# One AdaLN transformer kernel: the down product in three split passes for eight more units, and its weights split a chunk earlier

## The reference, cut to what matters

```python
scores = softmax(xf @ router_w)                     # 8 experts, the two best are kept
g = einsum('nh,ehf->enf', xf, gate_w)
u = einsum('nh,ehf->enf', xf, up_w)
y = einsum('enf,efh->enh', silu(g) * u, down_w)
routed = einsum('enh,ne->nh', y, combine)
shared = silu(xf @ shared_gate_w) * (xf @ shared_up_w) @ shared_down_w
return shared + routed
```

## Time and profile before

| | us |
|---|---|
| median of 3 runs | 518.63 (518.32 to 519.63) |
| the profiled execution, whole | 518.72 |
| its span | 516.9 |
| TensorE busy | 501.3 (97%), 1941 instructions |
| VectorE busy | 423.4 (82%) |
| ScalarE busy | 390.3 (76%) |
| GpSimd busy | 261.7 (51%) |

### The profile page before, as it was taken

How to read it: one execution, slowest core, us unless ns; L and a number is a source line. 1 busy time by engine, 2 the same in 40 slices (tenths; PEclk the granted TensorE clock), 3 DMA queues, 4 the chain that set the end, 5 groups by cost and what they waited for, 6 DMA issues and landing times.

```text
span 516.9 us, 8074 instructions
## 1 busy us (share of the span) xinstructions
PE 501.3 (97%) x1941; PEld 300.4 (58%) x1941; DVE 423.4 (82%) x1624; ACT 390.3 (76%) x586; POOL 261.7 (51%) x307
## 2 busy tenths in 40 slices
PE   8789999999999999999999999999989999999997
PEld 6345555555555555555555555555546576666675
DVE  5888888988898888888888888898888566876854
ACT  4768888888888888888888888888888753445353
POOL 3445555556656566655555665656655530213242
PEclk9999999999999999999999999999999999999999
DMA  8200010001000100100010001000000000707070
GB/s 246 96 16 1 7 42 15 0 5 41 15 5 15 25 15 5 31 25 0 5 41 15 0 5 41 15 5 21 20 1 1 1 1 1 178 6 184 1 183 22
DMA packets 19526, 17.51 MB, mean 34 GB/s; under 512 B 8604, under 2 KB 14236, under 8 KB 19508
## 3 DMA queue, kind: packets, MB, share of 16 engines
q1 hardware_dynamic: 18644, 16.58, 12.6%
q10 hardware_dynamic: 864, 0.73, 0.4%
HBM read 9.96 MB, written 1.05 MB: 21 GB/s over the span
## 4 chain that ended last, share of the span: by engine, by line
PE 87%; DVE 5%; POOL 3%; issue 2%; ACT 2%; DMA 1%; DVEq 0%; POOLq 0%
PE bank L449 19%; PE bank L440 15%; PE bank L315 12%; PE bank L462 6%; PE bank L607 5%; PE bank L437 5%; PE bank L357 4%; PE bank L362 4%; PE bank L358 4%; PE bank L564 3%; PE bank L563 3%; PE bank L565 3%; DVE hf L1079 1%; PE bank L561 1%; DVE stI L1043 1%
## 5 line engine op out<-in xcount | busy, mean ns | idle before, releaser
L449 PE MATMUL bank<-hid,wf 128*128 128x512 f32 x256 | 120.2, 592 | 0.0
L941 POOL TENSOR_TENSOR rsD<-veD,c_half 128x4 f32<-128x4 f32 x32 | 37.8, 1180 | 118.1 <-DVE veD L1060 118.1
L440 PE MATMUL bank<-x,wf 128*128 128x512 f32 x192 | 93.0, 593 | 0.0
L775 ACT ACTIVATE hid<-bank,vbf 128x512 f32<-128x512 f32 x128 | 77.6, 693 | 1.9 <-PE bank L440 1.9
L449 PEld LDWEIGHTS bank<-hid,wf 128*128 128x128 f32 x256 | 46.1, 190 | 46.6 <-issue 31.3
L440 PEld LDWEIGHTS bank<-x,wf 128*128 128x128 f32 x192 | 35.0, 189 | 33.4 <-issue 16.3
L1150 DVE TENSOR_SCALAR x<-bank,vln 128x256 f32<-128x256 f32 x64 | 31.8, 540 | 23.8 <-PE bank L315 23.8
L1079 DVE TENSOR_SCALAR xhB<-bank,meanB,rsB 128x128 f32<-128x128 f32 x128 | 43.7, 405 | 9.1 <-POOL rsB L941 9.1
L1079 DVE TENSOR_SCALAR xhD<-bank,meanD,rsD 128x128 f32<-128x128 f32 x128 | 43.7, 404 | 7.1 <-POOL rsD L941 2.9
L745 ACT ACTIVATE g<-bank,vbf 128x512 f32<-128x512 f32 x31 | 21.4, 689 | 35.8 <-PE bank L449 35.8
L315 PEld LDWEIGHTS bank<-ident,y 128*128 128x128 f32 x256 | 29.4, 140 | 26.4 <-POOL y L961 12.8
(11 more groups left out here) (185 smaller groups left out, 1118.4 us busy)
## 6 DMA issues: line engine op xcount, KB each, us to landing
wf<-in_w_f SPq DMA_DIRECT2D x16, 256.0 KB, 2.6
hid<-kv_full SPq DMA_DIRECT2D x12, 256.0 KB, 4.3
x<-kv_full SPq DMA_DIRECT2D x9, 256.0 KB, 5.0
wu<-in_w_unit SPq DMA_DIRECT2D x10, 192.0 KB
wqkv<-in_w_qkv SPq DMA_DIRECT2D x7, 192.0 KB, 2.4
x<-in_x SPq DMA_DIRECT2D x4, 256.0 KB, 5.4
qk<-kv_full SPq DMA_DIRECT2D x3, 256.0 KB, 5.0
out<-ot SPq DMA_DIRECT2D x3, 256.0 KB, 2.2
```

Of the source, the lines that this page charges most:

```text
L440: mm = nc.tensor.matmul(ps_ff[j][:], wf1[:, j * P:(j + 1) * P], x2[(c - 2) % CH][:], start=True, stop=True)
L449: mm = nc.tensor.matmul(ps_f0[:], wf2[:, j, :], hid[:, j, :], start=(j == 0), stop=(j == FJ - 1))
L775: nc.scalar.activation(hid[:, j, :], ps_ff[j][:], ACT.Gelu_apprx_tanh, bias=vbf1[:, j:j + 1]).then_inc(h_ready, 1)
L941: nc.gpsimd.tensor_tensor(rs[buf(k, n)][:], ve[buf(k, n)][:], c_half[:], ALU.pow).then_inc(rstd_ready[k], 1)
```

## The change

Down products of the first eight units of the third chunk (units 20 to 27) are done in three passes as well. So split(i) gives 0 to 7 for them, and 8 to 15 for those of the fourth chunk; ScalarE and GpSimd write the high and low parts of 16 instead of 8 tiles sc. The down weights are split in the iterations of the second chunk (c == CH - 3 is c == 1) instead of the third.

```diff
         def split(i):
 
-            return i - (CH - 1) * U if (CH - 1) * U <= i < CH * U - 2 else -1
+            c, u = divmod(i, U)
+            return (c - CH + 2) * (U - 2) + u if c >= CH - 2 and u < U - 2 else -1
...
-                if c == 2 and u < U - 2:
+                if c == CH - 3 and u < U - 2:
                     nc.scalar.activation(wu_hi[:, u, 2, :], wu[:, u, 2, :], ACT.Copy).then_inc(wd_hi_ready, 1)
...
-                if c == 2 and u < U - 2:
+                if c == CH - 3 and u < U - 2:
                     pool.wait_ge(wd_hi_ready, u + 1)
                     nc.gpsimd.tensor_tensor(wu_lo[:, u, 2, :], wu[:, u, 2, :], wu_hi[:, u, 2, :].bitcast(F32),
                                             ALU.subtract).then_inc(wd_lo_ready, 1)
```

## The result

The changed kernel takes 524.5 us (median of 5 runs, 524.23 to 526.26), the kernel before 518.6 (518.32 to 519.63). The ratio is 1.0117, 95% interval 1.0103 to 1.0131: slower by 1.2%. The forecast was 522.4 us, range 520.6 to 524.8. Direction and place were right; the size was 2.1 us short.

A forecast was written before the change was run, and what follows sets the result against it. TensorE, busy 97% of the span, was taken as the bound. Terms of +3.7 and +0.2 us at kk made +3.9, taken as +3.8 on 518.63: 522.4 us, range 520.6 to 524.8.

The forecast's parts named there:

- Three passes: Down products of units 20 to 27: period 2.265 to 2.10 us, -1.32 us in all, -0.50 ahead of the xhF transposes.
- Low parts cost no wait by themselves: New operands: low part ready 0.57 us before its pass, so no wait where nothing else is queued on GpSimd.
- Low part 23 ahead of rsF: Fourth chunk's norm: GpSimd makes rsF late, xhF transposes start 3.8 us later, TensorE stands for 4.3 us.
- the 1.4 named as a sign: Sign in the profile after: VectorE's first product of unit 23 takes 1.4 us.
- From xhF to kk: Between the fourth chunk's xhF and kk transposes: VectorE decides, sum at kk +3.7 us, TensorE waiting some 0.5 us there.
- Weights' splits: Splits moved to the second chunk: hidden except for a conflict with VectorE's first product of unit 17, +0.2 us.
- Fourth chunk: Fourth chunk's buffers, waits and order stay: 0 us.
- The clock: Rival, chance 0.19: TensorE's clock falls in the stall before the xhF transposes, +1.5 us, so 523.9 us.
- the forecast case: Main case, chance 0.72: late rsF stalls TensorE before the fourth chunk's xhF transposes, 522.4 us, 0.7% slower.
- The rule of the Trainium skill quoted there: Rule: a matmul stream that keeps waiting for data drops to half rate and begins the next burst cold; 523.9 us by it.
- RsF has cover: Rival, chance 0.09: at the fourth chunk's norm nbias is less than 1.3 us late, saved passes come through, 517.3 us.
- the point named: Deciding point for covered rsF in the fourth chunk's norm: rsF starts before 474.3.

The follow-up runs named there:

- the stop filled: Changed kernel with 16 float32 128x128 matmuls put on TensorE ahead of the wait for the fourth chunk's xhF: 523.03 us, 1.0086 to the kernel before.
- the low part of hf moved ahead: Changed kernel, GpSimd making the fourth chunk's rsF and nbias ahead of low part 23 and its low part of hf ahead of low part 26: 520.29 us.
- the one tried with all eight: Changed kernel with fourth-chunk norm and low part of hf earlier on GpSimd, statistics and kk earlier on VectorE, units 20 to 27 in three passes: 520.58 us.
- the kernel with rsF ahead: Changed kernel, but GpSimd makes rsF and nbias of the fourth chunk ahead of the low part of unit 23: 520.56 us, 1.0036 to the kernel before.

## Why the prediction held where it did, and what it missed

The 5.70 us of kk to kk split by the experiments: 2.67 us from the place of low part 23 (16.02 - 13.35), 0.71 us left of the way to xhF, 1.57 us from the clock (15.45 - 13.88), and 0.75 us left of the way from xhF (13.88 - 13.13). Each part is a difference of two profiled executions. Outside that stretch there are 0.2 us more.

1. *Three passes.* Right: period 2.10 us, 0.47 us saved ahead of xhF for 0.50 (up 25 ends so much earlier, counted from kk).
2. *Low parts cost no wait by themselves.* Right in the fourth chunk and in units 20 to 22: no wait of TensorE for a low part there.
3. *Low part 23 ahead of rsF.* Right in place and chain; rsF at 477.26 (477.1 forecast), sc of unit 23 late by 0.96 us for 0.75. The stop was 3.68 us for 4.3, xhF +3.41 us for +3.8. Nbias started 1.16 us after rsF, not 1.61, since rsF took 1.01 us, not 1.46. I had taken over the length from before, where VectorE's product of unit 23 (two SBUF inputs) ran beside rsF; here VectorE had nothing to do by then. (In every trace looked at rsF takes 1.46 to 1.50 us with such a product beside it and 1.01 to 1.02 without one.) And the conflict with low part 22 fell on veF, two instructions earlier than I put it; the first product of unit 23 took 0.68 us, not the 1.4 named as a sign. The Trainium skill (SBUF — State Buffer, Who interferes with whom) says that a VectorE instruction with two SBUF inputs contends with a GpSimd instruction that reads SBUF. It names no size, and I had applied it to the large products alone. The trace agrees, with 1.28 us for a 128x4 instruction.
4. *From xhF to kk.* The failing step. The forecast left VectorE 3.7 us late at kk; it was 5.7. Of the 2.0 us between them 1.6 are the clock's: with the stop filled VectorE is 4.13 us late. I put the conflict with the low part of hf at 0.65 us. The three subtractions in a row held VectorE off twice, 0.81 us at ex and 1.03 us at unit 28. TensorE's wait at kk, for which I had allowed less than 1 us, became 1.51. I had asked which low part meets which product, but not what VectorE meets when GpSimd has the next subtraction ready as the last one ends. That step alone was 1.2 us short. It shows as only 0.4 us at kk because other terms were too dear: the first product of unit 26 came some 0.5 us earlier than I had it, and 0.25 us was made up ahead of unit 29, where VectorE had idled before (0.28 us). With the low part of hf moved ahead both conflicts are gone in the profiled execution (12.43 us from xhF), though most executions of that kernel are 1 to 2 us slower than that would give.
5. *Weights' splits.* Right: +0.17 us for 0.2, of which 0.07 came back in the third chunk.
6. *Fourth chunk.* Right: from kk to the end 26.90 us, before 26.83.

*The clock.* I gave it 0.19 at 523.9 us, and the forecast case stood on its staying up. It fell, in the profiled execution for some 3.4 us, and cost 1.57 us, for 1.5 in the rival. That the two are so near is partly luck: I had 4.0 us at half clock less a slack of 0.5 us, where 3.4 us (1.7 us of work) reached the path almost whole. Passes were 0.43 us apart, not 0.47. So the case that came true was this rival; its own miss was 0.6 us, and the range held because it made room for the rival, not because the forecast case was right. Against a stop twice as long as any before, a chance of 0.19 was low. The rule of the Trainium skill quoted there agrees with this trace in that the clock fell behind the stop, but not in that the next burst begins cold: the first microsecond ran at 1.00. *RsF has cover:* fell; it started 3 us past the point named. *The range:* its own terms make 521.5 to 523.4 us, not the 521.2 to 523.6 that I wrote; nothing hangs on it.

What the change could have brought came through for six of the eight units, 0.99 of the 1.32 us: with the low parts kept out of the way of the two places where TensorE waits, kk to kk fell by 1.45 us, a fifth of it from a wait that the change had not touched. For units 22 and 23 no order that pays was found; the one tried with all eight lost 0.83 us.

## What to carry to other kernels

When work is added to an engine that is idle half the time, ask what stands behind it in that engine's program and who waits for that, not whether there is room. An operand that is made late in an iteration belongs behind everything that the next stage waits for. And price a new stop of TensorE with the clock in it: the stop cost 3.4 us here, and the clock behind it 1.6 more.

## What the runs showed of the hardware

- The granted clock fell to 0.50 behind a wait of TensorE of 3.68 us and also, in one of five executions for certain, behind 2.17 us. It was still 1.00 for 1.1 and 1.3 us after TensorE had resumed, and stayed down for some 3.4 us in the one case and 6.8 in the other.
- In other executions it fell in the kernel's first 36 us: at about 29 us in four profiled ones, which cost 0.9 to 1.2 us by the third chunk's kk; at about 9 us, for some 7 us, in one, which cost 1.2 us; and at just under 10 us in three, which cost nothing (kk for the third chunk at 464.2 to 464.3). The waits did not decide it: in the kernel with rsF ahead TensorE waits 0.18, 0.92 and 0.73 us at 26 to 29 us and the clock falls, and in the kernel before it waits just as long there and the clock stays at 1.00.
- In the stretches at 0.50 a weight load takes 0.33 us instead of 0.19. It takes 0.33 us in the first 5.7 us of the kernel too, where the profile gives the clock as 1.00.
- A VectorE instruction of 4 elements per partition was held for 1.1 us by a GpSimd subtraction. When GpSimd had two subtractions in a row, VectorE's small product got through as the first ended, GpSimd's second started at the same moment (490.70), and VectorE's next product waited for all of that: it ended at 492.54, 0.54 us after the second.
- It goes the other way as well: in the profiled execution of the kernel with the low part of hf ahead, a GpSimd subtraction and a VectorE product started together at 487.12, the product took its usual 0.69 us and the subtraction 1.84 instead of 1.29.
